# Attention with masks on the vector engine and far rows inside the bands, and a new order of the down products

## What is computed

```python
scores = jnp.einsum('bhqd,bhkd->bhqk', Q, K) * scale        # B=8, 16 heads, S=512, d_head=16
scores = scores + longformer_mask(S)                        # open: |i - j| <= 64, or i == 0, or j == 0
out = jnp.einsum('bhqk,bhkd->bhqd', softmax(scores), V)
x = x + out @ Wo + bo
...
topk_weight, topk_idx = jax.lax.top_k(scores, C)            # 16 experts, C = 512 of 4096 rows each
g, u = xg @ Wg.T, xg @ Wu.T                                 # 256 -> 1024
eo = (gelu(g) * u) @ Wd.T                                   # 1024 -> 256, weighted, scatter-added
```

## Time and profile before

| what | value |
|---|---|
| median of 3 runs | 1398.01 us (1396.7 to 1398.82) |
| the profiled execution | 1400.23 us, its span 1398.5 us |
| busy: PE, DVE, ACT, POOL | 1256.7, 849.4, 597.1, 584.9 us |
| project | to about 104 us, its last store to 110 us |
| attend | 110 to 517 us |
| front | 517 to about 800 us |
| experts | about 800 to the end |
| mean granted clock of PE | 0.952 of 2.4 GHz |

### The profile page before, as it was taken

How to read it: one execution, slowest core, us unless ns; L and a number is a source line. 1 busy time by engine, 2 the same in 40 slices (tenths; PEclk the granted TensorE clock), 3 DMA queues, 4 the chain that set the end, 5 groups by cost and what they waited for, 6 DMA issues and landing times. The chain is left out here.

```text
span 1398.5 us, 26404 instructions
## 1 busy us (share of the span) xinstructions
PE 1256.7 (90%) x9930; PEld 1066.7 (76%) x9930; DVE 849.4 (61%) x1510; ACT 597.1 (43%) x1023; POOL 584.9 (42%) x530
## 2 busy tenths in 40 slices
PE   2995999999999972699999599999999999999997
PEld 2884777777777752588887578888888888888886
DVE  7874555555555512695688676666666666666641
ACT  1340544444444442354222255455455454545442
POOL 6000333332333342462200146666666666665554
PEclk9996999999999985699999789999999999999999
DMA  2778555555555416441003144434444433344411
GB/s 84 262 249 136 79 88 90 86 86 92 93 93 93 71 50 198 144 149 57 15 31 121 51 161 121 115 105 113 120 121 121 121 111 105 109 114 121 121 31 15
DMA packets 71284, 148.44 MB, mean 106 GB/s; under 512 B 14736, under 2 KB 31520, under 8 KB 64928
## 3 DMA queue, kind: packets, MB, share of 16 engines
q1 hardware_dynamic: 58544, 128.39, 35.4%
q0 software_dynamic: 12656, 18.90, 7.4%
HBM read 104.53 MB, written 42.21 MB: 105 GB/s over the span
## 5 line engine op out<-in xcount | busy, mean ns | idle before, releaser
L610 ACT ACTIVATE pt<-ps_p 128x512 f32<-128x512 f32 (+1 forms) x320 | 170.0, 582 | 218.1 <-PE ps_x L673 122.7
L550 DVE TENSOR_REDUCE mx<-ps_s 128x2 f32<-128x384 f32 (+2 forms) x160 | 143.9, 900 | 171.9 <-PE ps_x L651 154.9
L1803 POOL TENSOR_TENSOR h_lo<-h,h_hi 128x512 fp32r<-128x512 f32 x128 | 175.5, 1383 | 136.1 <-ACT h_hi L1839 135.8
L454 POOL TENSOR_SCALAR_AFFINE_SELECT pt<-pt 128x512 f32<-128x512 f32 x192 | 110.1, 597 | 273.4 <-ACT pt L610 273.4
L1913 PE MATMUL ps_gu<-xt_hi,w_hi 128*128 128x512 f32 x512 | 203.5, 397 | 2.1 <-DVE xt_lo L1862 2.1
L1913 PE MATMUL ps_gu<-xt_lo,w_hi 128*128 128x512 f32 x512 | 200.8, 392 | 0.0
L1913 PE MATMUL ps_gu<-xt_hi,w_lo 128*128 128x512 f32 x512 | 200.3, 391 | 0.0
L1878 DVE TENSOR_TENSOR h<-ge,ps_gu 128x512 f32<-128x512 f32 x128 | 87.8, 686 | 180.1 <-ACT ge L1833 167.9
L1740 DVE TENSOR_TENSOR w_lo<-w,w_hi 128x768 fp32r<-128x768 f32 x128 | 173.5, 1360 | 31.3 <-ACT w_hi L1735 27.8
L648 PE MATMUL ps_s<-ks,qs 96*128 96x256 f32 (+2 forms) x512 | 171.6, 398 | 0.0
L1812 POOL DMA_INDIRECT out<-ys,idx x64 | 131.1, 2049 | 73.3 <-ACT ys L1849 61.8
(11 more groups left out here) (221 smaller groups left out, 2891.9 us busy)
## 6 DMA issues: line engine op xcount, KB each, us to landing
w<-in_We SPq DMA_DIRECT2D x48, 1024.0 KB, 4.9
qk_parts<-qk SPq DMA_DIRECT2D x8, 2048.0 KB, 7.7
qs<-qk_parts SPq DMA_DIRECT2D x96, 128.0 KB, 3.6
ks<-qk_parts SPq DMA_DIRECT2D x96, 128.0 KB, 5.0
x<-in_x SPq DMA_DIRECT2D x16, 512.0 KB, 8.7
attn_t<-on SPq DMA_DIRECT2D x32, 256.0 KB, 3.7
ot<-attn_t SPq DMA_DIRECT2D x32, 128.0 KB
rd<-rden SPq DMA_DIRECT2D x16, 256.0 KB
```

Source lines behind the costliest of these rows:

```text
L454: last = pool.affine_select(out=part, in_=part, pattern=[[0, HQ], [sign, hi - lo]], compare_op=ALU.is_ge, fill=0.0, base=0, channel_multip ...
L550: last = dve.tensor_reduce(mxu[:, h:h + n, j], tile[:, :, 0:N0 if j == 0 else W[j]], AX, ALU.max)
L610: act.activation(pt[i][:, t % 2, h:h + nh], ps_p[:, n % 2].rearrange("p (h q) -> p h q", h=nh)[:, :, 0:W[i]], ACT.Exp, scale=SCALE).then_i ...
L1803: pool.tensor_tensor(h_lo[:, m], h32[:, (e * KI + m) % HB], h_hi[:, m].bitcast(F32), ALU.subtract).then_inc(hlo_s, 1)
```

## The change

In `project`, `qk` is kept with 129 columns per 128 queries, and POOL copies column 0 of the first tile into each 129th column, so that query 0 and key 0 stand behind every tile. SP waits for that copy and stores with eight DMAs a batch, in rows of 516 values, one per part and feature half. The weights of q and k are permuted on the host so that one step's rows of one part lie together.

In `attend`:
- A score is one matmul of one head into one of three banks (`RING = 3`), over 512, 258, 258 or 194 columns, with key 0 inside. The mask matmuls and the two-column matmuls go. DVE adds the mask and takes the maximum in one `tensor_tensor_reduce` per head and query tile: 16 a step. The four merging and far instructions go.
- An exponent job is two heads in two banks: eight jobs a step instead of ten, query 0 in the band, no two-column matmuls and no exponent of its own. Key tile 0 keeps its mask.
- Two of the 129th columns of the maximum rows have to be filled: ACT copies them (`far_rows`) for step u + 1 in step u, between exponents 5 and 6, once the four `m_rows` DMAs have landed.
- `times_v` stands in two pairs, behind exponent jobs 5 and 7. Its last tile takes two matmuls a head instead of one. POOL masks in 11 selects of 64 columns a step instead of 6 of up to 128.
- SP issues four loads, four `m_rows` and one store a step: nine instead of eleven. The copy-out of step u - 2 comes after exponent 0. All loops are unrolled.

In `experts`, the down products take blocks 0 to 6 of tile 0, blocks 0 to 6 of tile 1, then block 7 of tile 0 and of tile 1, then tiles 2 and 3; before them stands one wait for the eviction of the last tile of the expert before.

```diff
 # project: SP, POOL
-                    sp.wait_ge(qlo_s, b * 4 + 4)
-                    sp.dma_start(d["qk"][b].rearrange("c (m p) q -> p c m q", p=P),
-                                 qk[:, h].bitcast(F32)).then_inc(out_s[h], 16)
+                    sp.wait_ge(z_s, b + 1)
+                    for c in range(4):
+                        for m in range(KD):
...
+                            sp.dma_start(dst, qk[:, h, c, m].rearrange("p k i -> p (k i)").bitcast(F32)).then_inc(out_s[h], 16)
+                for b in range(B):
+                    pool.wait_ge(qlo_s, b * 4 + 4)
+                    rows = qk[:, b % 2].rearrange("p c m k i -> p (c m) k i")
+                    pool.tensor_copy(rows[:, :, :, P], rows[:, :, 0, 0:1].to_broadcast([P, 4 * KD, NT])).then_inc(z_s, 1)
 # attend: POOL
+                def near_only(u, i):
+                    pool.wait_ge(exp_s, u * SJ + 2 * (i + 1))
+                    for n in range(W[i] // WIN):
...
+                        last = pool.affine_select(out=part, in_=part, pattern=[[0, HQ], [sign, WIN]], compare_op=ALU.is_ge,
+                                                  fill=0.0, base=sign * (n % 2) * WIN, channel_multiplier=-sign)
+                    last.then_inc(sel_s, 1)
 # attend: SP
+                for u in range(NU):
+                    b, t = u // UB, u % UB
+                    if u + 1 < NU:
+                        m_rows(u + 1)
+                    if u + UB < NU:
+                        sp.wait_ge(st_s, (u + 1) * SJ)
+                        load(u + UB)
+                    if u >= 1:
+                        store(u - 1)
+                    if b >= 1 and t == 1:
+                        load_den(b - 1)
+                    if b >= 1 and t == 3:
+                        store_rden(b - 1)
 # attend: DVE
+                    for g, (j, h) in enumerate(SCORES):
+                        dve.wait_ge(sc_s, u * SG + g + 1)
+                        n, m = (S, mask[:, 0:S]) if j == 0 else (WZ[j], mask[:, S:S + WZ[j]])
+                        dve.tensor_tensor_reduce(junk[:, (u * SG + g) % RING, 0:n], ps_s[:, (u * SG + g) % RING, 0:n], m, 1.0, -3e38, ALU.add, ALU.max,
+                                                 mx[:, u % 2, h, j:j + 1]).then_inc(mx_s, 1)
 # attend: ACT
+                def far_rows(u):
+                    t = u % UB
+                    act.wait_ge(m_in[t], (u // UB + 1) * 16 * MROWS)
...
+                for u in range(NU):
+                    for n, (i, p) in enumerate(TJOBS):
+                        act.wait_ge(st_s, u * SJ + n + 1)
+                        if n == 0 and u >= 2:
+                            act.wait_ge(av_s, u - 1)
...
+                        act.activation(dst, src, ACT.Exp, scale=SCALE).then_inc(exp_s, 1)
+                        if n == 0 and u >= 2:
+                            out_rows(u - 2)
+                        if n == 5 and u + 1 < NU:
+                            far_rows(u + 1)
 # attend: PE
+                def score(u, g):
...
+                    if n >= RING:
+                        pe.wait_ge(mx_s, n + 1 - RING)
...
+                    pe.matmul(out, q, k, start=True, stop=True).then_inc(sc_s, 1)
+                def exponents(u, n):
...
+                    if n == 0:
+                        pe.wait_ge(far_s, u + 1)
+                    if u * SJ + n >= 2:
+                        pe.wait_ge(exp_s, u * SJ + n - 1)
...
+                for u in range(NU):
+                    for n in range(SJ):
+                        if u + 2 < NU:
+                            score(u + 2, 2 * n)
+                            score(u + 2, 2 * n + 1)
+                        exponents(u, n)
+                        if u >= 1 and n in (5, 7):
+                            times_v(u - 1, n - 5)
+                            times_v(u - 1, n - 4)
 # experts: PE
-                    for t in range(CT):
-                        if e > 0 or t >= 2:
-                            pe.wait_ge(ys_s, e * CT + (t - 1))
...
+                    if e > 0:
+                        pe.wait_ge(ys_s, e * CT)
+                    contract(0, range(KI - 1))
+                    contract(1, range(KI - 1))
+                    contract(0, range(KI - 1, KI)).then_inc(y_s, 1)
+                    contract(1, range(KI - 1, KI)).then_inc(y_s, 1)
+                    for t in range(2, CT):
+                        pe.wait_ge(ys_s, e * CT + (t - 1))
+                        contract(t, range(KI)).then_inc(y_s, 1)
```

More of the change, by code:

```diff
@@ L51 @@
 M_ROW = 96
+RING = 3
+ZC = P + 1
+ZS = NT * ZC
 LO = [0] + [P * i - WIN for i in range(1, NT)]
@@ L57 @@
 W = [h - l for l, h in zip(LO, HI)]
+WZ = [w + 2 for w in W]
+SIDE = ZC + 1
+FAR = [0, WIN + SIDE, WIN, WIN]
+UPPER = [0, SIDE, SIDE, ZC]
 def three(h_l, h_r, l_l, l_r):
@@ new lines, in score @@
+                    if n >= RING:
+                        pe.wait_ge(mx_s, n + 1 - RING)
+                    q = tile_of(qs[0:M_ROW, t, h], j)
+                    k = ks[0:M_ROW, t, h]
+                    k = whole(k) if j == 0 else window(k, j)
+                    out = ps_s[:, n % RING]
+                    out = out.rearrange("p (k c) -> p k c", c=P) if j == 0 else out[:, 0:WZ[j]]
+                    pe.matmul(out, q, k, start=True, stop=True).then_inc(sc_s, 1)
+                def exponents(u, n):
+                    b, t = u // UB, u % UB
+                    i, p = TJOBS[n]
+                    if n == 0:
+                        pe.wait_ge(far_s, u + 1)
+                    if u * SJ + n >= 2:
+                        pe.wait_ge(exp_s, u * SJ + n - 1)
+                    if i == 0:
+                        for r in range(2):
+                            pe.matmul(ps_p[:, n % 2, r, 0:N0], ident16[:], mask[:, 0:N0], start=True, stop=False,
+                                      skip_group_check=True)
+                    for r in range(2):
+                        k = tile_of(ks[:, t, 2 * p + r], i)
+                        q, out = qs[:, t, 2 * p + r], ps_p[:, n % 2, r]
@@ L675, in st_job, with near @@
                     last.then_inc(st_s, 1)
-                def times_v(b, t, i, first):
+                def near(rows, v, p, i):
+                    out = ps_o[rows, LO[i]:HI[i]]
+                    if i < NT - 1:
+                        pe.matmul(out.rearrange("p (k c) -> p k c", c=WIN), v,
+                                  p.rearrange("p (k c) -> p k c", c=WIN + 1)[:, :, 0:WIN],
+                                  start=False, stop=True, skip_group_check=True)
+                    else:
+                        pe.matmul(out[:, 0:WIN], v, p[:, 0:WIN], start=False, stop=True, skip_group_check=True)
+                        pe.matmul(out[:, WIN:W[i]], v, p[:, WIN + 1:W[i] + 1], start=False, stop=True, skip_group_check=True)
@@ L698, in times_v @@
                                              skip_group_check=True)
                         else:
-                            last = pe.matmul(ps_o[rows, 0:1], v, pq[:, t % 2, h, i - 1:i], start=False, stop=True,
+                            z = FAR[i]
+                            last = pe.matmul(ps_o[rows, 0:1], v, pt[i][:, s, h, z:z + 1], start=False, stop=True,
                                              skip_group_check=True)
```

360 lines of the change are left out of this document (132 added, 228 removed).

## The result

The changed kernel takes **1618.73 us** (1616.25 to 1620.4), the kernel before beside it 1398.41 us: ratio 1.157, interval 1.154 to 1.160. It is slower by 220 us, where the prediction had 42 us less. The profiled execution took 1620.4 us, its span is 1618.7 us.

The account below looks back on a forecast made before the run. PE was taken to set attend's 12.10 us step. Attend 32 us (42 - 12 + 2), experts 11 and project -1.5 gave 41.5 us off 1400.2, 1358.7, less 2.2 for the median: 1356 us, range 1330 to 1392 us.

Parts of the forecast that it names:

- Part 5: Start of attend and project: 2 us gained at attend's start; project's extra stores cost 1.5 us, ends 0 and 8 us.
- A: Project's store, theory from the experiments, not the prediction: the destination's outermost dimension, 2, holds a DMA to two of 16 engines.
- (c): Experts or project: tile 0's eviction eats the new order's gain, or project loses 8 us; 1363 to 1367 us; 7%.
- (d): Attend: the new DVE instruction at half rate or with a large fixed cost makes DVE the bound; 1491 us; 9%.
- Part 1: Attend: PE's own work falls to 8.6 us in a step of 12.1 us; removed matmuls are 3.5 us.
- Part 2: Attend: 16 new DVE instructions take 7.6 us a step, bounds 6.5 and 8.9 us.
- Part 3: Attend, PE and DVE meshing: DVE late, idle 1.8 and 0.65 us behind product pairs; step 10.7 us, 42 us saved.
- Part 4: Attend: ACT's wait for the maximum rows costs nothing in normal steps, 1.7 us in seven fourth steps, 12 us.
- (a): Attend: PE's fourth-step stalls lower the clock, costing some 2 us in the step behind, 14 us; 1370 us; 15%.
- Part 6: Experts: the new down order removes PE's wait for the low part; net 0.7 us x 16 = 11 us gained.
- (b): Attend: scores waiting for their bank restart their weights, 0.9 to 1.8 us a step; 1383 us, up to 1395 us; 13%.
- (e): Attend: better case, 6.5 us of DVE work and no fourth-step stall, 1311 us; half of it 1333 us; 10%.

Follow-up runs that it names:

- e3: Kernel before with 8 stores a batch in project instead of one, each to 128 joined rows of 2048 bytes: 1400.58 us, ratio 0.999.
- e1: Changed kernel with project's store cut into 4 DMAs a batch, one per quarter of the heads, 64 partitions to 64 joined rows: 1336.24 us, ratio 0.953.
- e10: e1 with the score masks back on PE as matmuls and a plain maximum on DVE: 1352.24 us, ratio 0.964.
- e8: e1 with the value products one behind each of jobs 4 to 7 instead of in two pairs: 1337.72 us, ratio 0.955.
- e9: e1 with SP's wait for the store of the reciprocals moved ahead of the next load of the denominators: 1325.41 us, ratio 0.947.
- e4: Kernel before with only the new order of the down products in experts: 1391.33 us against 1400.79 us, ratio 0.9926.
- e2: Kernel before with 8 stores a batch in project, each to two groups of 64 rows of 2048 bytes kept apart by padding: 1666.05 us, ratio 1.189.

## Why the prediction was wrong

**Part 5, project: the step that failed.** It says "Bytes are the same, packets too" and names DMA at 0.83 as the cover that hides eight issues. Bytes and packets were right and beside the point, and that eight issues are hidden was right as well (e3). The step priced a DMA by its bytes and its issue, and took the 286 GB/s of the earlier trace rows for granted in the new form. But those were reached by a store whose outermost dimension is the 128 partitions, and the diff's is `t d h q` with two values of t, which by A is on 2 of the 16 engines. Worked out by A: a batch stores 8 x 264 KB at 50 GB/s, 42 us, and loads x behind it, 46 us against 9.4 us; eight of them are 293 us. The upper end for this term (8 us) named two mechanisms, slower rows of 516 and a late x. Both are there. The rows and their layout cost some 8% of the rate (47 against 51 GB/s) and, with all else that is new in project, at most the 6.9 us of e1. The x is late, but by up to 36.9 us in a batch, for a reason that the step didn't have, and not by 1 us. Of the rivals (c) had a loss in project, of 8 us, and the slower one (d) was about DVE, so the range missed by 227 us. The rate that a DMA of the new shape reaches was the unknown, and the prediction gave it no bound of its own.

**Part 1, PE's own work: near.** 8.6 us a step; e10 gives an estimated 8.2 us or less.

**Part 2, DVE: 1.3 us a step too much.** 0.61, 0.35 and 0.28 us stand for 0.67, 0.43 and 0.37, 6.3 us in sum for 7.6 us. That is even under the lower bound of 6.5 us: the row of the closest operation was dearer than the new one, and the fixed part of the new one is smaller (0.61 us less 512 x 0.94 ns is 0.13 us, for 0.19 us). The 7.1 us that the prediction estimated from the Trainium skill (VectorE: DVE Perf Modes, the TRN2 errata) are above the measured 6.3 us too. (d) is refuted.

**Part 3, the mesh: the idle times right, their role not.** DVE is idle for 1.71 us and 0.74 us behind the two pairs, for 1.8 us and 0.65 us. With part 2's number put right the sum is 6.3 + 0.6 + 1.7 + 0.74 = 9.3 us, of 9.74 us measured, for 10.7 us. That such a sum comes out doesn't make the pairs the cause of the period, as the prediction had it: e8 took the pairs apart, and the step stayed within 0.09 us. What sets the 9.74 us isn't shown. Part 3 also counted 30 steps alike. The last four store-to-store distances gained nothing (42.9 us for 42.2 us): in 740 to 748 us the clock was 0.50, where in the like products before (500 to 508 us) it was 1.00.

**Part 4: the mechanism right, the size about double.** The wait for the reciprocals' store delays `far_rows` in the fourth steps, with 4.32 us of idle on ACT in one of them:

```profile
555.29 0.21 ACT L587 ACTIVATE qs<-qs 2x8 fp32r<-2x8 f32 x1 [4.32 <-DMA qs<-mt]
```

It cost 0.4 to 2.0 us in each of the first six fourth steps, 6.0 us together, where the prediction had 1.7 us each and 12 us in seven; e9, whose fourth steps are like the others, shows the wait to be the only cause. Rival (a), a lower clock behind these stalls, came true behind one of them (0.66 in 677 to 682 us, behind the step of 11.71 us): the step after it took 10.43 us, 0.7 us more than normal, where the rival had 2 us.

**Part 6, experts: right.** 0.7 us an expert, 11 us; e4 gives 10 us by itself. **Blocked scores (b):** PE does wait for maxima, 4.9 us in four steps of e1, in 24 weight loads of 0.2 us. But that is part of its slack, and not 0.9 to 1.8 us on top of a step: the sum of part 3 leaves 0.4 us for everything that it doesn't have.

With the store put right (e1) the forecast of 1356 us stands against 1336 us. In e1's profile attend gave 62 us, 30 us more than the 32 us of the sum, project cost 6.9 us instead of 1.5 us, and front, which is untouched, took 3.5 us more than before: 21 us together. Rival (e), 6.5 us of DVE work and no stall in the fourth steps, comes nearest: 1333 us for half of it. Its first half is there in e1 (6.3 us), its second in e9.

## What to carry to other kernels

When a diff reshapes a DMA, write out both access patterns as the instruction will carry them, with joined dimensions joined, and look at the outermost size before bytes, packets or issues; a leading dimension of 2, 4 or 8 held the stores here to 51, 102 and 202 GB/s. In a profile the mark is a stretch where all engines are idle, the DMA share is low and the issuing queue spends microseconds on each DMA: a bound transfer that doesn't look busy. And a wait on a queue costs what is queued behind it: moving one wait of SP past the maximum rows gave about 10 us, of which 5 us are placed, and spreading PE's products gave nothing.

## What the runs showed of the hardware

- The rate of a store followed the number of groups in its destination: 51, 102 and 202 GB/s for 2, 4 and 8 groups of rows, with 0.13, 0.26 and 0.53 of the DMA engines busy. With one block of 128 rows project as a whole ran at 270 GB/s.
- Issuing holds the queue when DMAs can't drain: 5.3 us for one store in the changed kernel, 0.4 us before.
- Rows of 2064 bytes in the new layout went at 47 GB/s in two groups, rows of 2048 bytes at 51 GB/s in e2's. In e1 the DMA engines were busy for 0.87 at 248 GB/s, before for 0.78 at 270 GB/s. What of this is the length of the rows, what the layout and what e1's strided stores (1.5 us of issue each) isn't shown; all of it together costs at most the 6.9 us of e1's later end of project.
- Adding a bf16 mask from SBUF to scores in PSUM and taking their maximum costs DVE what the plain maximum costs: 0.69, 0.42 and 0.36 us each for 512, 258 and 194 columns (rows of L549 above), and these are e10's plain maxima (busy us, mean ns of one):

```profile
L549 DVE TENSOR_REDUCE mx<-ps_s 128x1 f32<-128x258 f32 x72 | 26.9, 422 | 2.1
L549 DVE TENSOR_REDUCE mx<-ps_s 128x1 f32<-128x512 f32 x38 | 24.5, 686 | 10.1 <-PE ps_s L628 10.1
...
L549 DVE TENSOR_REDUCE mx<-ps_s 128x1 f32<-128x194 f32 x40 | 12.5, 355 | 18.1 <-PE ps_s L628 17.7
```
